# Moving the exponential out of PSUM and the query transposes behind the value product, in a fused attention and mixture-of-experts kernel

## The reference

```python
h = layernorm(x) * (1 + ca) + sa
q, k, v = split(h @ W_qkv)            # per head
q, k = rope(q), rope(k)
q_feat = elu(q * SCALE) + 1.0         # = max(q, 0) + exp(min(q, 0))
k_feat = elu(k) + 1.0
kv = einsum('bhtd,bhtv->bhdv', k_feat, v)      # summed over all tokens
k_sum = k_feat.sum(axis=2)
out = einsum('bhtd,bhdv->bhtv', q_feat, kv) / max(q_feat . k_sum, 1e-6)
x = x + ga * (out @ W_out)
```

## Time and profile before

| what | value |
|---|---|
| profiled execution | 678.13 us |
| its span | 676.0 us |
| median of 3 executions | 678.13 us |
| PE busy | 568.7 us (84%) |
| DVE busy | 456.5 us (68%) |
| ACT busy | 320.0 us (47%) |
| POOL busy | 269.0 us (40%) |
| TensorE clock, mean | 0.93 of full |

### The profile page before, as it was taken

How to read it: one execution, slowest core, us unless ns; L and a number is a source line. 1 busy time by engine, 2 the same in 40 slices (tenths; PEclk the granted TensorE clock), 3 DMA queues, 4 the chain that set the end, 5 groups by cost and what they waited for, 6 DMA issues and landing times.

```text
span 676.0 us, 13788 instructions
## 1 busy us (share of the span) xinstructions
PE 568.7 (84%) x4041; PEld 529.4 (78%) x4041; DVE 456.5 (68%) x1304; ACT 320.0 (47%) x717; POOL 269.0 (40%) x427
## 2 busy tenths in 40 slices
PE   4999889998997101279999999999999999999990
PEld 3577668887776000169999999999999999999990
DVE  3577889897677877867756766567667666666431
ACT  3688778886444500034534534445345444454330
POOL 5688757776678000302007025043070160442304
PEclk9999999999999555569989999999999999999996
DMA  5322268545554900144408317344174073340203
GB/s 164 94 64 78 71 194 264 189 145 162 157 190 153 264 0 0 40 133 133 133 1 213 94 44 170 95 141 102 61 198 106 18 194 95 110 102 9 32 1 39
DMA packets 91911, 75.24 MB, mean 111 GB/s; under 512 B 12108, under 2 KB 88278, under 8 KB 91864
## 3 DMA queue, kind: packets, MB, share of 16 engines
q1 hardware_dynamic: 82872, 58.77, 28.6%
q0 software_dynamic: 8992, 15.90, 11.2%
HBM read 52.48 MB, written 22.16 MB: 110 GB/s over the span
## 4 chain that ended last, share of the span: by engine, by line
PE 59%; DVE 13%; issue 7%; POOL 3%; ACT 2%; DMA 2%; DVEq 1%; SPq 0%; ACTq 0%; POOLq 0%
PE bank L1329 33%; PE bank L1341 15%; PE bank L1247 3%; PE bank L1292 2%; DVE hit L880 2%; PE bank L1150 2%; PE bank L1306 1%; DMA mod_all<-mod_store 1%; DVE x L847 1%; DVE st L849 1%; POOL out L506 1%; PE bank L1227 1%; PE bank L1236 1%; DMA xg<-h_rows,g_idx 1%; PE bank L1202 0%
## 5 line engine op out<-in xcount | busy, mean ns | idle before, releaser
L1329 PE MATMUL bank<-xT_h,w_h 128*128 128x320 f32 x512 | 160.2, 313 | 2.3 <-DVE xT_l L1027 1.7
L1329 PE MATMUL bank<-xT_l,w_h 128*128 128x320 f32 x512 | 159.2, 311 | 0.4 <-issue 0.4
L1329 PE MATMUL bank<-xT_h,w_l 128*128 128x320 f32 x512 | 159.0, 311 | 0.0
L496 POOL DMA_INDIRECT xg<-h_rows,g_idx x40 | 43.8, 1095 | 274.5 <-DVE g_idx L999 264.7
L1055 DVE TENSOR_TENSOR hid<-act_g,bank 128x320 f32<-128x320 f32 x128 | 62.0, 484 | 74.1 <-ACT act_g L648 59.6
L652 ACT CAST hid_h<-hid 128x320 fp32r<-128x320 f32 x128 | 58.9, 460 | 97.5 <-DVE hid L1055 92.8
L648 ACT ACTIVATE act_g<-bank 128x320 f32<-128x320 f32 x128 | 55.8, 436 | 103.3 <-PE bank L1329 96.2
L1329 PEld LDWEIGHTS bank<-xT_h,w_h 128*128 128x128 f32 x512 | 97.6, 191 | 3.0 <-DVE w_l L1013 2.1
L1329 PEld LDWEIGHTS bank<-xT_h,w_l 128*128 128x128 f32 x512 | 97.5, 190 | 0.5 <-issue 0.5
L1329 PEld LDWEIGHTS bank<-xT_l,w_h 128*128 128x128 f32 x512 | 97.5, 190 | 0.5 <-issue 0.5
L1341 PE MATMUL bank<-w_h,hid_h 128*128 128x256 f32 x320 | 91.4, 286 | 0.4 <-DVE hid_l L1060 0.4
(11 more groups left out here) (180 smaller groups left out, 1118.2 us busy)
## 6 DMA issues: line engine op xcount, KB each, us to landing
w_raw<-wg SPq DMA_DIRECT2D x32, 256.0 KB, 3.3
w_raw<-wu SPq DMA_DIRECT2D x32, 256.0 KB, 4.4
w_raw<-wd SPq DMA_DIRECT2D x16, 512.0 KB, 6.1
x_in<-x SPq DMA_DIRECT2D x32, 128.0 KB, 2.1
q_store<-qT SPq DMA_DIRECT2D x32, 128.0 KB, 1.9
q_in<-q_store SPq DMA_DIRECT2D x32, 128.0 KB, 2.2
x_re<-x SPq DMA_DIRECT2D x32, 128.0 KB, 2.2
out<-x SPq DMA_DIRECT2D x32, 128.0 KB, 1.9
```

Source lines behind the costliest of these rows:

```text
L496: nc.gpsimd.indirect_dma_start(out=xg[par][:, a, :], out_offset=None, in_=h2_rows, in_offset=bass.IndirectOffsetOnAxis(ap=g_idx[par][:, a: ...
L1329: last = MM(bank[2 * h + m][:, 0:HCAP], W[i][:, f, at:at + P], XT[j][:, k, cols], start=n == 0, stop=n == 3 * KC - 1)
```

## The change

`ex` becomes a tile of its own in SBUF. The q transposes write to bank 5 instead of bank 4, and so the two waits between them and the transposes of the normed tile go. On TensorE the q transposes move behind the value product; on ScalarE the copy `qT` moves from ahead of `neg` to behind the last place of `copy_v`.

```diff
-        neg, feat = sa("neg", [P, 2 * D]), sa("feat", [P, 2 * D])
+        neg, ex, feat = sa("neg", [P, 2 * D]), sa("ex", [P, 2 * D]), sa("feat", [P, 2 * D])
...
-        qT_ps = bank[4][:, D:2 * D]
-        ex = bank[5][:, :]
+        qT_ps = bank[5][:, 0:D]
...
 # ScalarE
-                if on["kv"]:
-                    wait(act, tr_q, s.t(-1))
-                    wait(act, st_q[s.par(-2)], s.half(-2) * 16)
-                    nc.scalar.copy(qT[s.par(-2)][:, :], qT_ps).then_inc(qT_d, 1)
                 if on["feat"]:
...
-                    nc.scalar.activation(ex, neg[:, :], ACT.Exp, scale=-1.0).then_inc(exp_d, 1)
+                    nc.scalar.activation(ex[:, :], neg[:, :], ACT.Exp, scale=-1.0).then_inc(exp_d, 1)
...
                 if on["qkv"] and on["att"]:
                     copy_v(s)
+                if on["kv"]:
+                    wait(act, tr_q, s.t(-1))
+                    wait(act, st_q[s.par(-2)], s.half(-2) * 16)
+                    nc.scalar.copy(qT[s.par(-2)][:, :], qT_ps).then_inc(qT_d, 1)
...
 # VectorE
-                    V.scalar_tensor_tensor(feat[:, :], rot[s.par(-1)][:, :], 0.0, ex, ALU.max, ALU.add).then_inc(feat_d, 1)
+                    V.scalar_tensor_tensor(feat[:, :], rot[s.par(-1)][:, :], 0.0, ex[:, :], ALU.max, ALU.add).then_inc(feat_d, 1)
...
 # TensorE
                     wait(pe, hT_d, s.t(1))
-                    wait(pe, qT_d, min(s.rep - 2, 0) if s.rep < 3 else s.t(-2))
                     for k in range(KC):
                         last = TR(hT_ps[:, k, :], hn[:, k * P:(k + 1) * P], ident[:, :])
...
-                if on["kv"]:
-                    wait(pe, feat_d, s.t(-1))
-                    wait(pe, qT_d, s.t(-2))
-                    if on["trh"]:
-                        wait(pe, hT_d, s.t(2))
-                    for k in range(KC):
-                        last = TR(qT_ps[:, k * P:(k + 1) * P], feat[:, k * P:(k + 1) * P], ident[:, :])
-                    last.then_inc(tr_q, 1)
-                if on["qkv"]:
                     wait(pe, v_done, s.t(0))
                     product(v_ps, (hT_h[s.par(0)], hT_l[s.par(0)]), (wqkv_h, wqkv_l), slice(2 * D, 3 * D))\
                         .then_inc(qkv_done, 1)
                 if on["kv"]:
+                    wait(pe, feat_d, s.t(-1))
+                    wait(pe, qT_d, s.t(-2))
+                    for k in range(KC):
+                        last = TR(qT_ps[:, k * P:(k + 1) * P], feat[:, k * P:(k + 1) * P], ident[:, :])
+                    last.then_inc(tr_q, 1)
                     wait(pe, v_done, s.t(-1))
```

## The result

The changed kernel took 685.50 us in the median of four executions (685.27 to 685.80), the kernel before 678.09 beside it. Over all 31 executions of the changed kernel (682.99 to 687.78) the ratio is 1.0116, 95% interval 1.0096 to 1.0137. Timed again later the ratio was 1.0107 (1.0078 to 1.0137). It is slower, as forecast, but by 7.4 us where 3.8 had been worked out.

What follows compares the result with a forecast made beforehand. Bound: a four-engine loop (3.44 us a step) with the first pass alone, TensorE with both passes. 678.13 + 2.1 (first stretch) + 1.2 (between) + 1.0 (both passes) - 0.5 (`attT`) = 681.9 us; range 676.2 to 686.5.

Steps and rivals of the forecast that it cites:

- the mechanism and the sign: VectorE's features with two SBUF tensors and GpSimd instructions stream in turn, the second waits; slower, 681.9 us, chance 0.52.
- The half rate: Features on two SBUF sources at half throughput: 0.53 us more in eleven steps, 687.7 us, chance 0.02.
- what the order is worth: Steps with the first pass alone: value product leaves the loop, 0.11 us a step gained, 1.2 us in eleven steps.
- what is late next: Steps with the first pass alone: after the new order GpSimd sets the pace with 3.33 us a step.
- the first stretch: Steps with the first pass alone: GpSimd loses 0.30 us, step 3.63 instead of 3.44, +2.1 us (-1.2 to +4.8).
- between the stretches: Around 91 us: features held 0.7 us by a long `rot`, 0.5 for steps around it; +1.2 us (0 to 3).
- the term for the stretch with both passes: Features wait some 0.35 us for `h`, hold `rot` some 0.3; 0.1 us in ten steps, +1.0 us (0 to 3).
- The 0.5 us to be taken back from `attT`: Both passes: `attT` has one copy fewer ahead on ScalarE, TensorE waits less; 0.5 us gained (0 to 1.5).
- paid in full, and VectorE becomes the bound there: Rival: full price of taking turns, VectorE's spare 0.5 us a step exceeded with both passes; 687.9 us, chance 0.12.
- The order wins: Rival: features fall into GpSimd's pauses, taking turns costs nothing; 676.4 us, chance 0.21.

Runs made afterwards that it cites:

- The order alone: Changed kernel with `ex` back in PSUM bank 5, q transposes in the free half of bank 1, one more wait: ratio 0.9957, on another chip 0.9974.
- `rot_b` less: Changed kernel with the second multiplication of `rot_b` on VectorE left out in the steps with both passes: ratio 1.0108.
- `bn_stats` less: Changed kernel with VectorE's two `bn_stats` looking at 16 columns instead of 256 in the steps with both passes: ratio 1.0071.
- the opposite experiment: Changed kernel with one VectorE instruction repeated: `bn_stats` in steps 18 to 28, 686.48 us; or a `rot_b` multiplication in steps 18 to 31, 684.29 us.
- less work on GpSimd: Changed kernel with GpSimd's multiplication `xm` handling one column instead of 256 in the steps with both passes: ratio 1.0199.

## Why the prediction was right and where it was wrong

**Right: the mechanism and the sign.** Features with two SBUF tensors and GpSimd's instructions take turns; the instruction itself is no slower. The changed kernel shows it in nearly every step, and the kernel with `ex` alone moved has the loss without the orders. The half rate, which the prediction left out of its sum, is not there: 0.69 us on two SBUF sources.

**Nearly right: what the order is worth, and what is late next.** Forecast: the value product leaves the loop and GpSimd's 3.33 us stop the gain. The order alone runs at 3.30 and wins 2.0 us to the 15th features, where 1.2 had been worked out. That 3.30 lies so near 3.33 is in part luck. The step read as having "no slack inside" had 0.12 us of it, ahead of `rot`: GpSimd's chain runs at 3.21 where it never waits, and every other step is 0.2 longer for VectorE's `rot_b`. The count of eleven steps is one too many as well; 38.33 and 72.71 lie ten apart.

**Right: the first stretch.** Forecast 3.63 us a step and +2.1 us (+1.9 by ten steps); measured 3.65 and +1.7. GpSimd's 3.21 and the 0.44 that `rs` is held give the 3.65; in the prediction's terms, 0.44 in place of its 0.30, less the 0.12 of slack.

**Too small: between the stretches.** Forecast 1.2, measured 2.5, and 2.2 in the second profile. The prediction priced one pair of features and put 0.5 on the rest. The five features from the 15th on take 1.27 to 1.65 us in place of 0.69, 4.0 us in all. How much of that the transfers of `mod_all`, which are on the chain in this stretch, hide, no run shows. The two runs of the order alone differ by 1.3 us here (24.39 and 23.12), as much as the whole miss.

**The step that failed: the term for the stretch with both passes.** It said that the features wait 0.35 us, that VectorE's spare 0.5 us a step "takes up 0.35 nearly", and took 0.1 us in each of ten steps, 1.0, less 0.5 for `attT`. Measured: 2.8 us in both profiles of the changed kernel, 2.3 of the 3.6 us that the forecast is short. The wait itself was read rightly in kind (features 0.5 us longer, `rot` 1.26 to 1.74). Wrong was to hold it against VectorE's mean slack. A wait of one engine for another is also an edge: the features hang on `h`, `h` hangs through `ve` on what VectorE does behind the features, and that round takes 5.5 us whatever slack stands elsewhere. Half of it was there to be read before: `rs` waited for `ve` in every step. That the turn with `h` costs these 3 us is shown by moving `ex` in these steps alone; that the loop is the reason is the reading that fits all the runs, `rot_b` less and `bn_stats` less above all, but the opposite experiment leaves it short of proven.

The 0.5 us to be taken back from `attT` was wrong in sign too. Waits from 108 to 160 us (us in total, times, longest), first of the kernel before, for which the earlier trace rows has `attT` with 1.5 us, then of the changed one:

```profile
POOL rs L465 <- DVE ve L728: 8.8, 10, 1.5
ACT hn L570 <- POOL sh L450: 1.4, 2, 0.9
```
```profile
ACT hn L569 <- POOL sh L449: 6.7, 8, 1.9
PEld bank L1241 <- ACT attT L588: 4.5, 6, 1.9
```

TensorE waits more for `attT`. `hn`, ahead of it on ScalarE, waits for GpSimd's `sh`, which stands behind the stretched `rot`. It isn't the order that does this: TensorE waits 1.9 and 2.3 us for `attT` in the two runs of the order alone, and 4.6 with `ex` alone in SBUF. So the order gave nothing back, and the place of `ex` cost more.

**Of the rivals,** "paid in full, and VectorE becomes the bound there" came nearest in time (687.9) and named the place, yet not the mechanism: a VectorE with 0.33 us less to do was as slow. "The order wins" is real as an effect, 2 us, and drowned.

**Left open.** The last two columns of the table, -0.9 and +1.4 us, lie in code that the change doesn't touch. The forecast had them at 0, and 0.5 us of the 7.4 is their sum. From the lookup to the end the second profile of the changed kernel took 396.0 us, 4.4 less than the first, and all the profiles, whatever was changed, lie between 396.0 and 402.0. So the +1.4 can't be told from what this stretch does by itself. Whether another loop than L's could give 5.5 us a round was not tested.

## What to carry to other kernels

Before a VectorE operand is moved out of PSUM, look at whether the other tensor operand is in SBUF and what GpSimd does at that time: with both in SBUF the two engines took turns here, and the one that came second paid, 0.2 to 0.5 us each time and up to 0.96 (features of 1.65). Price such a turn as an edge between two queues and follow it round, through every wait that leads back, not as so much slack used. And don't trust a chain that names one busy engine before its instructions have been compared with their own length alone: it was the wait inside them. Keeping one operand in PSUM, and the q transposes in a half bank that was free, kept the gain of the new order.

## What was not expected of the hardware

GpSimd's `rs`, one number per partition, takes 0.55 us and became 1.00, although it reads two numbers per partition and writes one. Why it needs the turn for so little stays open. In the changed kernel it is held in the steps where the features stream first; where they started 0.21 us after it, both kept their lengths:

```profile
23.85 0.55 POOL L446 TENSOR_TENSOR rs<-ve,half_neg 128x1 f32<-128x1 f32 x1
24.06 0.69 DVE L827 SCALAR_TENSOR_TENSOR feat<-rot,ex 128x512 f32<-128x512 f32 x1 [1.19 <-ACT ex L583]
```

And less work on GpSimd made the kernel slower by some 6 us (1.0199 against 1.0107 to 1.0116), while the same edit cost the kernel before nothing (1.0001). What the timelines show beside it is another order in which the two engines arrive; no run isolates it.
